# Two cross-attentions in one kernel: a pair's product whole in the second step of its group

## What is computed

```
q = split_heads(normed @ wq); k = split_heads(ctx @ wk); v = split_heads(ctx @ wv)
scores = einsum('bhqd,bhkd->bhqk', q, k)
ctx = einsum('bhqk,bhkd->bhqd', softmax(scores), v)
x1 = hidden_states + ctx.reshape(b, q_len, 1024) @ wo
...
scores = einsum('brd,bfd->brf', x1, ctx_1024)
out = x1 + einsum('brf,bfd->brd', softmax(scores), ctx_1024)
```

## Time and profile before

| | |
|---|---|
| median of 3 runs | 595.46 us (590.26 to 595.83) |
| the profiled execution | 591.87 us |
| its span, first to last instruction | 590.1 us |
| TensorE busy (matmuls) | 566.5 us, 96% |
| VectorE, ScalarE, GpSimd busy | 454.3, 392.7, 457.0 us |
| mean granted TensorE clock | 0.994 |

### The profile page before, as it was taken

One profiled execution on the slowest core, in us unless ns is written; L12 is line 12 of the kernel. 1 busy time (PEld: TensorE's weight loads), 2 busy tenths in 40 slices (PEclk: granted clock), 3 DMA queues, 4 the chain that ended last, 5 costly groups with the idle time before them and its releaser, 6 DMA issues.

```text
span 590.1 us, 10838 instructions
## 1 busy us (share of the span) xinstructions
PE 566.5 (96%) x3748; PEld 514.6 (87%) x3748; DVE 454.3 (77%) x641; ACT 392.7 (67%) x520; POOL 457.0 (77%) x532
## 2 busy tenths in 40 slices
PE   7889999899999999999999999999999999999896
PEld 7678889798999889988999899998999898988795
DVE  5678789679876898779876988778877898778413
ACT  5677667658666876767666777667766677667602
POOL 3337886987789987997879987997879897998800
PEclk9999999999999999999999999999999999999989
DMA  6076847656566767576666767676666766756300
GB/s 223 1 173 157 215 111 191 174 148 165 154 168 171 205 156 183 151 195 162 156 168 169 204 159 178 154 193 164 153 169 177 200 159 161 177 151 174 88 5 5
DMA packets 47808, 92.45 MB, mean 157 GB/s; under 512 B 14698, under 2 KB 20234, under 8 KB 47754
## 3 DMA queue, kind: packets, MB, share of 16 engines
q1 hardware_dynamic: 39834, 76.71, 51.3%
q10 hardware_dynamic: 7920, 15.05, 9.4%
HBM read 8.72 MB, written 0.41 MB: 15 GB/s over the span
## 4 chain that ended last, share of the span: by engine, by line
PE 55%; POOL 23%; DVE 8%; ACT 5%; issue 4%; SPq 3%; DMA 1%; ACTq 0%; POOLq 0%; DVEq 0%
PE ps_o L1205 24%; POOL turned_p L554 14%; PE ps_s L1094 8%; PE ps_s L1096 8%; PE ps_s L1095 8%; DVE neg_max L894 4%; POOL c_lo L559 4%; SPq L457 3%; PE ps_m L998 3%; PE ps_o L1201 2%; PE ps_m L1017 1%; DVE blocks L917 1%; ACT turned_p L720 1%; ACT probs L691 1%; POOL tails L543 1%
## 5 line engine op out<-in xcount | busy, mean ns | idle before, releaser
L554 POOL TENSOR_TENSOR turned_p<-turned_p 128x1408 fp32r<-128x1408 f32 (+1 forms) x109 | 339.1, 3112 | 10.0 <-ACT turned_p L720 7.9
L1205 PE MATMUL ps_o<-turned_p,c_hi 128*128 128x256 f32 (+2 forms) x1273 | 250.0, 292 | 2.5 <-POOL turned_p L554 1.2
L691 ACT ACTIVATE probs<-ps_s,neg_max 128x1444 f32<-128x1444 f32 (+1 forms) x109 | 160.0, 1468 | 136.0 <-DVE neg_max L894 134.4
L894 DVE TENSOR_REDUCE neg_max<-ps_s 128x1 f32<-128x1444 f32 (+1 forms) x111 | 184.3, 1660 | 83.2 <-PE ps_s L1096 82.2
L1205 PEld LDWEIGHTS ps_o<-turned_p,c_hi 128*128 128x128 f32 x1273 | 207.0, 189 | 4.9 <-issue 2.8
L1205 PE MATMUL ps_o<-turned_p,c_lo 128*128 128x256 f32 (+2 forms) x693 | 185.7, 270 | 0.0
L917 DVE STREAM_TRANSPOSE blocks<-probs 128x1408 f32<-128x1408 f32 (+1 forms) x109 | 178.1, 1634 | 2.0 <-DMA turned_p<-blocks 1.7
L720 ACT ACTIVATE turned_p<-turned_p 128x1536 fp32r<-128x1536 f32 (+1 forms) x109 | 156.3, 1435 | 4.1 <-DMA turned_p<-blocks 4.1
L1205 PEld LDWEIGHTS ps_o<-turned_p,c_lo 128*128 128x128 f32 x693 | 132.3, 191 | 0.0
L1094 PE MATMUL ps_s<-cT_hi,q_hi 128*128 128x512 f32 (+3 forms) x312 | 122.4, 392 | 1.9 <-DVE q_lo L800 1.8
L1096 PE MATMUL ps_s<-cT_hi,q_lo 128*128 128x512 f32 (+3 forms) x312 | 118.7, 380 | 0.0
(11 more groups left out here) (149 smaller groups left out, 444.0 us busy)
## 6 DMA issues: line engine op xcount, KB each, us to landing
turned_p<-blocks SPq DMA_DIRECT2D x667, 96.0 KB, 2.3
turned_p<-blocks ACTq DMA_DIRECT2D x141, 96.0 KB, 2.7
ctx_raw<-in_ctx_dram SPq DMA_DIRECT2D x8, 704.0 KB
turned_p<-blocks SPq DMA_DIRECT2D x40, 48.0 KB, 1.9
turned_p<-blocks ACTq DMA_DIRECT2D x24, 48.0 KB, 2.0
wq_sb<-in_L_xattn_wq_dram SPq DMA_DIRECT2D x2, 256.0 KB, 5.0
wk_sb<-in_L_xattn_wk_dram SPq DMA_DIRECT2D x2, 256.0 KB, 5.2
wv_sb<-in_L_xattn_wv_dram SPq DMA_DIRECT2D x1, 512.0 KB, 6.2
```

The lines of the kernel that those rows point to most:

```text
L554: pool.tensor_tensor(lo, lo.bitcast(F32), hi.bitcast(F32), ALU.subtract).then_inc(remainder, 1)
L691: act.activation(probs[step % 2][0:m, 0:S], score_tile(step, m), ACT.Exp, bias=neg_max[0:m, s:s + 1], accum_out=sums[0:m, s:s + 1]).then_i ...
L894: dve.tensor_reduce(neg_max[0:m, s:s + 1], score_tile(step, m), AX.X, ALU.max, negate=True).then_inc(maxed, 1)
L1205: t = pe.matmul(*todo[i], start=(i == 0), stop=(i == len(todo) - 1))
```

## The change

A pair has no product in the first of its two steps any more, and one part of one in the second. So in the first step TensorE goes from the scores over the bank writes of both places straight to the scores of the next step, and in the second it does L1201 and all 34 matmuls in a row. The late and the last unit, and `finished_at`, stay as they were: a pair is complete after the same step.

```
         b, g = group
         if g != ODD:
-            return ("pair", b, g), half, 2
+
+            return (("pair", b, g), 0, 1) if half else None
```

## The result

The changed kernel takes **610.61 us** (median of 6 runs, 606.85 to 613.13), the kernel before beside it 592.71 us (median of 6, 590.26 to 595.83). The ratio is 1.028 with a 95% interval of 1.025 to 1.032: slower by 17.9 us. The forecast was 600 us, with a range of 593.5 to 608. The direction was right and the size wrong.

What follows compares the result with a forecast made beforehand. TensorE, busy 566.5 of 590.1 us, was taken as the bound. Terms of 19.6 us lost and 11.9 us won gave 7.7 us more on 591.87, so 600 us, range 593.5 to 608.

Steps and rivals of the forecast that it cites:

- The clock at the new gaps: Behind the seven batch-boundary idle times of TensorE: granted clock stays 1.00, nothing added to the sum.
- rival 1: Clock falls behind all seven batch-boundary gaps, 9.8 us more, 609 us; chance 0.12.
- The clock behind the old wait: At 115.29, behind TensorE's 2.36 us wait: with that wait gone, 1.4 us of slow clock won back.
- The boundary: Seven batch boundaries: next scores wait 2.0 us for the context remainder `cT_lo`; 1.78 us each, 12.5 us lost.
- the restart: Behind each boundary wait, TensorE's first matmul is followed later than usual: 0.1 us each, 0.7 us lost.
- the end: Step 112: the second tile's transposes no longer have a half product ahead of them; 1.6 us lost.
- Waits of L1201 that go: The product's later start removes L1201's waits for GpSimd's remainder and VectorE's `o_norm`: 8.2 us won, plus 1.0 of restart.
- What GpSimd takes back: Late scores of step 10 wait for `x_lo` in batches 1, 2, 4, 6 and 7: 3.8 us lost.
- The context pieces of steps 11 and 12: With only one score block between these pieces, 0.1 us of wait, 7 times; 0.5 us lost with smaller ones.
- The start and the ordinary groups: Step 8's scores wait 0.5 us for step 6's exponential; in ordinary groups such waits are covered, priced at nothing.
- Rival 2: GpSimd isn't the bound, or the end and start are absorbed: loss 2 to 5 us, about 595; chance 0.31.
- Rival 3: At batch boundaries the context remainder is done 2 us sooner, so 12.5 + 0.7 us vanish: 586 us; chance 0.07.

Runs made afterwards that it cites:

- the fourth experiment: The changed kernel with 16 identity transposes put ahead of each batch-boundary wait; 603.0 us, 1.017 of the kernel before.
- e10: The changed kernel with the third context piece moved behind step 12's product, and group 1 and the last batch's group 3 in halves; 585.4 us, 0.986 of before.
- e1: The changed kernel with group 3's pairs in halves again, all others whole; 588.8 us, 0.993 of the kernel before.
- e3: The changed kernel, every pair whole, with the third context piece transposed behind step 12's product instead of step 13's scores; 589.0 us, 0.994 of before.

## Why the prediction was right in direction and wrong in size

The prediction's sum was 7.7 us over its own execution's 591.87 us. Split by the full clock, that was 19.6 lost and 10.5 won in structure, 9.1 net, and 1.4 won by the clock. Measured on the profiled pair: 11.4 us in structure, and 5.6 us lost by the clock. So the error of 9.3 us (608.86 - 599.6) is 2.3 us of structure and 7.0 us of clock. By the windows above the 7.0 are 5.1 at the boundaries, 1.7 at the start and 0.5 over an idle stretch, less 0.3, since the old wait gave back 1.7 and not 1.4.

*The clock at the new gaps: the step that failed.* The sum put the clock behind the seven new gaps at nothing. It stood beside the sum only as rival 1, with 0.12, for all seven or none. The argument against was that the one gap that had lost the clock followed output matmuls of 100 columns, while these follow a full score block. The runs show that this does not protect: behind gaps of 1.9 us the clock was 0.67 at three of seven places in the changed kernel, at three of six with group 3 alone whole, whose first gap of 2.28 us lost it too, and at 0.67 or 0.68 at three of seven with group 0 in halves. Each fall cost 1.7 us, 5.1 in the changed kernel's profile, and with the gaps filled there was none. That the clock falls behind the gaps was one of the prediction's own signs of being wrong. The right term would have been some of the seven, not none. Rival 1's mechanism was right, its all-or-nothing form wrong, and that its 609 us lie so near the 608.86 measured is luck: three gaps fell and not seven, and the rest came from the structure and the start. The Trainium skill (TensorE: Matmul & The Clock Gate, "HAM oscillation — how this bites in real kernels") has it that repeated idle gaps between bursts can make the engine fall back each time; these traces agree in part, with 0.67 behind three gaps and 1.00 behind four alike, and the filled gaps of the fourth experiment, 1.00 behind each, bear out the cause. Which gap falls is open: neither length nor what stands before it tells equal gaps apart here.

*The clock behind the old wait: right.* "With the wait gone I count 1.4 us back" came true, with 1.7: the clock is 1.00 where the product of 115.29 now stands. The five profiles with group 0 in halves (the kernel before, group 3 or group 1 alone whole, the move in the kernel before, the change with group 0 in halves) all have a wait of 2.36 to 2.63 us there and a slow stretch behind it; the eight with group 0 whole have neither.

*The boundary: right.* Predicted 2.0 us of idle at seven places, put down to `cT_lo`: 13.3 us in 7 places, 1.9 at the longest. The 0.06 us from the end of the remainder to the next matmul, which no row of the prediction gives, is 0.14 here (286.97 to 287.11). Together with the restart and the end 14.8 us were predicted for group 3, and 15.2 (undone in the change) and 13.2 (done alone) measured.

*Waits of L1201 that go: right.* Predicted to vanish: the row of L1202 has 0.8 us of idle before it, where it was 6.5 in the kernel before.

```profile
L1202 PE MATMUL ps_o<-turned_p,rinv_ones 128*128 128x256 f32 (+1 forms) x55 | 18.7, 341 | 0.8 <-POOL turned_p L555 0.6 <-DVE o_norm L869 0.2
```

*What GpSimd takes back: right in kind, somewhat small.* Predicted 3.8 us. Shown are 4.2 us in 5 places, in the batches that were named (1, 2, 4, 6 and 7), and with the 0.16 us hidden at each 5.0. The place that the earlier trace rows showed, in the changed kernel; the scores of step 9 end at 196.29 + 0.19 = 196.48 and `x_lo` is done at 197.35:

```profile
196.29 0.35 PE L1097 MATMUL ps_s<-cT_hi,q_lo 128*128 128x420 f32 x1
...
196.95 0.40 POOL L580 TENSOR_TENSOR x_lo<-x_T,x_hi 128x100 fp32r<-128x100 f32 x1
...
197.49 0.44 PE L1095 MATMUL ps_s<-cT_hi,x_hi 128*100 128x512 f32 x1 [0.85 <-POOL x_lo L580]
```

The forecast had both reasons, that group 1's half no longer stands between and that the waits in group 0 are gone; the runs with group 1 alone and with group 0 in halves bear out that the second is needed.

*The context pieces of steps 11 and 12: mis-sized.* Predicted 0.1 us each, 0.5 us in all. The weight loads of L1018 wait 3.0 us in 7 places, and giving group 2 its halves back was worth 1.0 to 1.6 us.

*The end: mis-sized.* Predicted 1.6 us from one product half of cover less the wait already there. The transposes now wait 2.48 us instead of 0.51, 2.0 us more, and about 2.2 us is what e10's halves there are worth, apart from the clock.

*The start and the ordinary groups: right.* Predicted 0.5 us for the start of batch 0, and nothing for ordinary groups. The one wait of the scores for an exponential in the whole trace is that of the start, 0.39 us and the 0.16 hidden:

```profile
51.28 0.50 PE L1095 MATMUL ps_s<-cT_hi,q_hi 128*128 128x512 f32 x1 [0.39 <-ACT probs L692]
```

The product matmuls kept their mean: 290 ns where the earlier trace rows has 292. That excludes a dearer product as the cause, as did e1.

*Rivals 2 and 3.* Rival 2 (the small prices stay small) fell: `x_lo` and the end came out larger than priced, not smaller. Rival 3 (the boundary is covered) gave 586 us for the case that it is; e3, where the remainder was moved under cover by another edit, took 589.0 and has a full-clock time of 586.8.

The structure's excess of 2.3 us (2.8 with the idle stretch at the end) is about what the three mis-sized terms give: 1.2 for `x_lo`, 0.5 to 1.1 for the context pieces and 0.4 to 0.6 for the end. What isn't settled is which of equal gaps loses the clock.

## What to carry to other kernels

Before work is moved off a place in an engine's order, read what else runs under it: the half product looked like plain work and was the cover of another engine's operation that the next step needed. Price a new idle gap of TensorE twice, its length and the slow stretch that may follow; here the seven gaps cost about 13 us by their length and about 7 by the clock, and the second part went when the gaps were filled with transposes that nothing reads. And try such a rule by groups: the same edit won 7 us in group 0 (594.1 to 586.7), cost 22.7 in group 3 (592.2 to 614.9), and groups 0, 4 and 6 alone beat the kernel before by 1.5%.

## What the runs showed of the hardware

Idle gaps of the same 1.9 us behind the same kind of work were followed by a granted clock of 0.67 or 0.68 over the next 5.2 us in nine of twenty cases (three of seven, of six and of seven in three kernels) and by 1.00 in the others; in two of the kernels it was the 4th, 5th and 6th, in the third others. The longest wait of L1201, 2.36 to 2.63 us, was followed by a low clock in five kernels of five. The wait of the end was no such sure case: 2.48 us in the changed kernel, with 0.76 behind it, and 2.47 us before the same transposes in the kernel with the early context piece, with 1.00 over 546.32 to 553.5. Each fall cost 1.7 us. Filling the seven gaps with 16 transposes each (13.8 us of busy time in all by the lines view) left the structure's time within 0.6 us and brought the clock's loss from 11.0 to 4.2 us. Run-to-run scatter is in good part the same thing: over six runs the changed kernel's times lie 6.3 us apart, but its full-clock times only 1.3 us; over 19 runs of the kernel before it is 6.3 and 3.1.
